# A fused attention and expert kernel: residual and router logits in one VectorE operation, GpSimd's power ahead of its scatters, first norms on ScalarE

## The chip, the cores and the metric

One core of one Trainium2 chip runs the whole program in one launch. The metric is the device time of that launch in microseconds. The engines named below are TensorE (PE in the profile, PEld for its weight loads), VectorE (DVE), ScalarE (ACT), GpSimd (POOL) and SyncE (SP), each with its own queue of instructions that it works through in order. Where one engine needs what another has made, it waits on a semaphore.

## The reference

The input x is 4 sequences of 1024 tokens of 128 numbers, float32. One layer is computed:

```
n  = layernorm(x)                       # over the 128 numbers, eps 1e-5
s  = (n Wq^T)(n Wk^T)^T / sqrt(1024)    # one head, causal
x1 = x + softmax(s) (n Wv^T) Wo^T
m  = layernorm(x1)
p  = softmax(m G^T)                     # 8 experts; the two best of each token
y  = sum over the two: p_e * (silu(m W1_e) * (m W3_e)) W2_e     # hidden width 256
out = x1 + y
```

## The kernel before

**Tiles and slots.** The 4096 tokens are 32 tiles of 128. The attention part runs in slots s = -3 to 31, one tile a slot, in two halves: tiles 0 to 15 are two sequences, 16 to 31 the other two. Within a half tile u has `blocks(u) = u % 16 // 2 + 1` blocks of 128 keys, so slots grow from 1 block to 8 and start again at 1 in slot 16. Wq and Wk are folded into one 128x128 matrix (`A_sb`) ahead of time, Wv, Wo and the router's weights into another (`M_sb`). Each engine's order is written out by hand, and the parts of one tile are spread over slots:

- PE, slot s: transpose of the normed tile s+3 (`transposes`, L536), scores of tile s+1 (L546, and the mask L547), projections of tile s+2 (`projections`, L559 and L560), transposes of the probabilities of tile s (`turn`, L569), in every fourth slot the ranks of a group of four tiles (L583 to L588), then probabilities times values of tile s-1 (`weigh`, L595). The last gives 136 columns: 128 of the attention's output and 8 that are its share of the router's logits.
- ACT, slot s: copies PSUM to SBUF: `XX` (L744, the transposed normed tile), `TL` (L749) and `xg` (L751, the logits' share of x itself, scaled by the standard deviation `sd1`), `PT` (L759), then the exponentials `Pr` of tile s+1 (L765, with a read of the row sum). PE's L559 of slot s waits for `XX` of slot s.
- DVE, slot s: for tile s-2 the reciprocal of the row sum (L879), the residual `X` (L885), the logits (L890, `gate`), mean and variance (L895, L899, `ve2` L903); for tile s+12 the first statistics (L850, L854; up to slot 19); for tile s+4 the first norm `xn` (L864); the negated maximum of the scores of tile s+1 (L874); the second norm of tile s-3 into `rows` (L911); the best experts (L917, L921); every fourth slot the routing of a group (L928 to L940) and a slot later the places of its rows (L948 to L982, ending in the semaphore `row_rdy`); in slots 22 to 26 also pieces of the list of expert tiles (L996 to L1024).
- POOL: the power -0.5 of the variances, four first ones at a time (`rstd1`, L398) and one second one a slot (`rstd2`, L402, for tile s-2), and the indirect DMAs that scatter the normed rows to the experts' stretches in DRAM (L451): 8 for each group of four tiles, queued in `waiting` when the group's places are known.

DVE's L911 in slot s needs `rstd2` of tile s-3, which POOL makes in its slot s-1. PE's `weigh` of tile u waits for the logits of tile u-1, since both use one PSUM bank.

**After slot 31** the expert part runs in 72 tiles of 128 rows: SP loads the rows, PE multiplies by W1 and W3 (L648) and W2 (L666), ACT makes silu (L781) and stages weights (L776), DVE multiplies (L1079, L1086), POOL scatters the results (L460), and at the end DVE adds them to `X` (L1197), which is written out.

## Time and profile before

| what | value |
|---|---|
| median of three runs | 292.99 us (292.64 to 295.81) |
| profiled execution | 293.88 us, its span 292.0 us |
| mean granted TensorE clock | 0.959 |
| attention part, up to the last `weigh` | from 0 to about 137 us of the span |
| expert part | from about 137 us to the end |
| PE, DVE, ACT, POOL busy over the span | 83%, 67%, 47%, 58% |
| L864 `xn`, 32 times | 10.8 us, mean 345 ns |
| L890 logits, 32 times | 7.0 us, mean 217 ns |
| L451 scatters, 64 times | 64.3 us, mean 1005 ns |
| L402 `rstd2`, 32 times | 19.1 us, mean 596 ns |

Busy shares are averages over stages that have different limits. The time of an instruction in a row is from its start to its end; on DVE and ACT the next one often starts before that end, so what an instruction costs its engine is the distance from its start to the next one's start. Idle time stands in square brackets behind a row, with what ended it.

### The profile page before, as it was taken

What the parts mean: (1) busy time and instruction counts of PE and PEld (TensorE: products, weight loads), DVE (VectorE), ACT (ScalarE), POOL (GpSimd) and SP (SyncE); (2) the same over time, 40 slices, a digit from 0 to 9 for tenths busy, and PEclk for the clock granted to TensorE, in tenths of its full rate; (3) what the DMA queues carried; (4) which work ended last, traced back from release to release, by engine and by line L of the source; (5) the groups of instructions that cost most, each with busy time, mean ns of one, the idle gap of its engine ahead of it and who ended that gap; (6) DMA issues with size and microseconds to landing.
All of it is one profiled execution on the core that took longest, in us unless ns stands there. A gap on an engine that the chain in (4) does not pass through costs nothing.

```text
span 292.0 us, 6399 instructions
## 1 busy us (share of the span) xinstructions
PE 241.4 (83%) x1769; PEld 209.5 (72%) x1770; DVE 195.0 (67%) x925; ACT 137.9 (47%) x369; POOL 169.1 (58%) x214
## 2 busy tenths in 40 slices
PE   7889999999698889798696788988979969899700
PEld 7767787788476767687595678878969858899600
DVE  4569998686788997685943289556464455597531
ACT  2256665575355555466743153455355354545100
POOL 5524388846868865627665745646556535475740
PEclk9999999999979999999988879999999999999975
DMA  7997011100101112201332224333222225751773
GB/s 215 322 339 208 3 38 46 39 28 30 38 28 38 50 46 61 72 19 39 89 82 65 67 69 112 92 94 83 74 77 82 73 56 147 228 193 37 236 243 108
DMA packets 31211, 28.96 MB, mean 99 GB/s; under 512 B 4168, under 2 KB 25680, under 8 KB 31184
## 3 DMA queue, kind: packets, MB, share of 16 engines
q1 hardware_dynamic: 25216, 18.80, 23.9%
q0 software_dynamic: 4352, 9.05, 9.0%
q10 hardware_dynamic: 1616, 0.79, 1.0%
q8 instruction: 12, 0.20, 0.3%
q14 instruction: 15, 0.12, 0.2%
HBM read 16.40 MB, written 12.22 MB: 98 GB/s over the span
## 4 chain that ended last, share of the span: by engine, by line
PE 56%; DVE 14%; issue 8%; POOL 6%; ACT 5%; another core or an unknown queue 4%; DMA 4%; SPq 1%; POOLq 0%; DVEq 0%
PE scores L648 9%; PE weighed L595 7%; PE turned L648 7%; PE weighed L666 7%; PE scores L546 7%; PE mixed L666 5%; POOL expert_rows L451 3%; PE scores L640 3%; PE turned L569 3%; PE mixed L559 3%; DVE ysb L1086 2%; PE mixed L560 2%; DMA TL<-L_attn_w_v 2%; DVE g L1079 2%
## 5 line engine op out<-in xcount | busy, mean ns | idle before, releaser
L460 POOL DMA_INDIRECT choice_rows<-ysb,ycol x72 | 71.4, 992 | 51.9 <-DVE ysb L1086 33.7
L451 POOL DMA_INDIRECT expert_rows<-rows,slots x64 | 64.3, 1005 | 30.2 <-issue 15.2
L776 ACT ACTIVATE Wt<-W 128x512 f32 x72 | 44.7, 625 | 13.8 <-issue 13.8
L648 PE MATMUL scores<-xT,Wt 128*128 128x128 f32 x288 | 41.2, 289 | 5.5 <-issue 4.7
L595 PE MATMUL weighed<-TL,PT 128*128 128x136 f32 x288 | 39.8, 283 | 3.6 <-DVE logit L890 2.4
L1071 DVE COPY xT<-scores 128x128 f32<-128x128 f32 x72 | 20.5, 285 | 32.8 <-PE scores L640 19.1
L648 PEld LDWEIGHTS scores<-xT,Wt 128*128 128x128 f32 x288 | 37.4, 203 | 6.9 <-issue 5.7
L595 PEld LDWEIGHTS weighed<-TL,PT 128*128 128x128 f32 x288 | 35.8, 191 | 4.7 <-issue 2.7
L648 PE MATMUL turned<-xT,Wt 128*128 128x128 f32 x288 | 38.5, 277 | 0.0
L546 PE MATMUL scores<-XX,TL 128*128 128x512 f32 (+3 forms) x96 | 37.6, 501 | 1.0 <-ACT TL L749 1.0
L648 PEld LDWEIGHTS turned<-xT,Wt 128*128 128x128 f32 x288 | 35.5, 194 | 0.0
L402 POOL TENSOR_TENSOR rstd<-ve,halves 128x1 f32<-128x1 f32 x32 | 19.1, 596 | 21.4 <-DVE ve L903 20.3
L666 PE MATMUL weighed<-w_sb,g 128*128 x148 | 25.0, 294 | 6.9 <-DVE ysb L1086 6.8
L781 ACT ACTIVATE sil<-turned 128x256 f32<-128x256 f32 x36 | 13.8, 383 | 35.4 <-PE turned L648 16.9
L749 ACT ACTIVATE TL<-mixed 128x264 f32<-128x264 f32 x32 | 12.5, 391 | 35.9 <-PE mixed L560 31.6
L765 ACT ACTIVATE Pr<-scores,negmax 128x128 f32<-128x128 f32 (+7 forms) x32 | 23.9, 747 | 7.1 <-DVE negmax L874 6.2
L666 PEld LDWEIGHTS weighed<-w_sb,g 128*128 128x128 f32 x148 | 20.5, 201 | 8.9 <-issue 8.7
L874 DVE TENSOR_REDUCE negmax<-scores 128x1 f32<-128x128 f32 (+7 forms) x32 | 23.5, 735 | 4.9 <-PE scores L547 3.7
L781 ACT ACTIVATE sil<-scores 128x256 f32<-128x256 f32 x36 | 13.7, 380 | 24.6 <-PE scores L648 16.9
L640 PE MATMUL scores<-identf,xt 128*128 128x128 f32 x72 | 19.9, 283 | 6.0 <-DVE xT L1071 6.0
L666 PE MATMUL mixed<-w_sb,g 128*128 x140 | 22.9, 287 | 2.4 <-DVE ysb L1086 1.9
L759 ACT ACTIVATE PT<-turned 128x512 f32<-128x512 f32 (+3 forms) x48 | 22.0, 491 | 3.1 <-PE turned L569 2.9
(145 smaller groups left out, 439.7 us busy)
## 6 DMA issues: line engine op xcount, KB each, us to landing
xt<-expert_rows SPq DMA_DIRECT2D x72, 66.0 KB
XX<-choice_rows SPq DMA_DIRECT2D x16, 256.0 KB
W<-L_ffn_w SPq DMA_DIRECT2D x2, 1024.0 KB, 9.6
choice_rows<-ysb,ycol POOLq DMA_INDIRECT x72
X<-L_attn_in_features SPq DMA_DIRECT2D x2, 512.0 KB, 8.0
expert_rows<-rows,slots POOLq DMA_INDIRECT x64
out<-X SPq DMA_DIRECT2D x4, 256.0 KB
expert_rows<-padrows SPq DMA_DIRECT2D x1, 528.0 KB
```

The source lines that it names most:

```text
L451: nc.gpsimd.indirect_dma_start(xs, bass.IndirectOffsetOnAxis(ap=slots[:, u, k:k + 1], axis=0), rows[:, u % ROWS_RING, k, :], None).then_in ...
L460: nc.gpsimd.indirect_dma_start(yb, bass.IndirectOffsetOnAxis(ap=ycol[:, q, 0:1].bitcast(u32), axis=0), ysb[:, q, :], None).then_inc(y_out[ ...
L546: mm(pS[u % 2][:, c:c + n * P], TL[:, u, 0:P], keys, start=True, stop=c + 512 < w)
L595: i = mm(pO[:, 0:VG], PT[:, u % 2, kt * P:(kt + 1) * P], TL[:, keys_of(u)[0] + PAIR * kt, P:], start=kt == 0, stop=kt == blocks(u) - 1)
L640: nc.tensor.transpose(bank[j % 2][:, 0:P], xt[:, j, 0:D], identf[:, :]).then_inc(xT_mm, 1)
L648: i = mm(bank[2 + j % RING][:, c * P:(c + 1) * P], Wt[:, j % RING, c * P:(c + 1) * P], xT[:, j % RING, :], start=True, stop=True)
L666: i = mm(product_bank(m, j)[:, 0:D], g[:, j % RING, c * P:(c + 1) * P], w2_sb[:, ds(w + c * D, D)], start=c == 0, stop=c == H // P - 1)
L759: copy(PT[:, u % 2, 4 * c * P:4 * c * P + w], pT[n % 2][:, 0:w], ACT.Copy).then_inc(pt_ev, 1)
L765: copy(Pr[:, u % 2, 0:w], pS[u % 2][:, 0:w], ACT.Exp, bias=negmax[:, u:u + 1], scale=1.0, accum_out=rowsum[:, u:u + 1]).then_inc(p_rdy, 1)
L776: copy(Wt[:, j % RING, :], W[:, ds(w * (SET // WIDE), SET)], ACT.Copy).then_inc(Wt_rdy, 1)
L781: copy(sil[:, j % RING, :], bank[2 + j % RING][:, 0:H], ACT.Silu).then_inc(sil_rdy, 1)
L874: v.tensor_reduce(negmax[:, u:u + 1], pS[u % 2][:, 0:blocks(u) * P], AX.X, ALU.max, negate=True).then_inc(max_rdy, 1)
```

## The change

Four things are done.

**1. One operation for residual and logits.** `X` gets rows of 136 columns; ACT writes `xg` into the last 8 of them, and one DVE operation adds all 136 columns. `gate` and the tile `logit` are gone. The semaphore `logit_rdy` is replaced by `x1_rdy`. Loads, stores and the last additions read the first 128 columns of each row.

**2. First norms on ScalarE.** The first four `xn` stay on DVE. The other 28 become an ACT operation, Identity with scale `rstd1` and bias `shift1` = -mean * rstd, at the end of ACT's slot (tile s+5, slots -1 to 26). DVE makes `shift1` for four tiles at once (L879 of the new file), beside `sd1`.

**3. GpSimd's power first.** `rstd_2` stands ahead of the slot's first scatter.

**4. Fewer scatters in short slots.** The second scatter of a slot (the one that waits for `pt_ev`) is made only where the slot has more than 4 blocks.

```diff
-        X = sb("X", [P, N_TILES, D])
+        X = sb("X", [P, N_TILES, VG])
...
+                if is_tile(s - X1_LAG):
+                    rstd_2(s - X1_LAG)
                 if waiting and is_tile(s):
                     pool.wait_ge(xx_ev, n_xx(s))
                     scatter(*waiting.pop(0))
-                if is_tile(s - X1_LAG):
-                    rstd_2(s - X1_LAG)
...
-                if waiting and is_tile(s):
+                if waiting and is_tile(s) and blocks(s) > 4:
                     pool.wait_ge(pt_ev, chunks(s + 1))
                     scatter(*waiting.pop(0))
...
-                wait(pe, logit_rdy, u)
+                wait(pe, x1_rdy, u)
...
-                copy(xg[:, u, :], pM[:, P + VG:P + VG + E], ACT.Copy, scale=sd1[:, u:u + 1]).then_inc(xg_rdy, 1)
+                copy(X[:, token_tile(u), D:], pM[:, P + VG:P + VG + E], ACT.Copy, scale=sd1[:, u:u + 1]).then_inc(xg_rdy, 1)
+
+            def norm1(u):
+
+                act.wait_ge(shift1_rdy, u // STAT1_GROUP + 1)
+                act.wait_ge(xx_mm, n_xx(u - 4 - XT_LEAD))
+                copy(xn[:, u % 4, :], X[:, token_tile(u), 0:D], ACT.Identity, bias=shift1[:, u:u + 1],
+                     scale=rstd1[:, u:u + 1]).then_inc(xn_rdy, 1)
...
                     exps(s + S_LEAD)
+                if s >= -1 and is_tile(s + NORM1_LEAD + 1):
+                    norm1(s + NORM1_LEAD + 1)
...
+                v.scalar_tensor_tensor(out=shift1[:, t], in0=mv1[:, t, 0], scalar=-1.0, in1=rstd1[:, t],
+                                       op0=ALU.mult, op1=ALU.mult).then_inc(shift1_rdy, 1)
...
-                v.scalar_tensor_tensor(out=X[:, token_tile(u), :], in0=pO[:, 0:D], scalar=rinv[:, u:u + 1],
+                dve.wait_ge(xg_rdy, u + 1)
+                v.scalar_tensor_tensor(out=X[:, token_tile(u), :], in0=pO[:, 0:VG], scalar=rinv[:, u:u + 1],
                                        in1=X[:, token_tile(u), :], op0=ALU.mult, op1=ALU.add).then_inc(x1_rdy, 1)
-
-            def gate(u):
-                dve.wait_ge(xg_rdy, u + 1)
-                v.scalar_tensor_tensor(out=logit[:, u, :], in0=pO[:, P:VG], scalar=rinv[:, u:u + 1],
-                                       in1=xg[:, u, :], op0=ALU.mult, op1=ALU.add).then_inc(logit_rdy, 1)
...
                     attend(u2)
-                    gate(u2)
...
-                if s >= 0 and is_tile(s + NORM1_LEAD):
-                    norm1(s + NORM1_LEAD)
-                    if (s + NORM1_LEAD) % STAT1_GROUP == 0:
-                        spread1(s + NORM1_LEAD)
+                if s == -S_LEAD:
+                    spread1(STAT1_GROUP)
+                u4 = s + NORM1_LEAD + 3
+                if u4 > STAT1_GROUP and is_tile(u4) and u4 % STAT1_GROUP == 0:
+                    spread1(u4)
```

How it moves instructions is seen in three places. The first is POOL in slots 15 and 16, before:

```order
L398 TENSOR_TENSOR rstd<-ve,halves 128x4 [waits ve1_rdy]
L451 DMA expert_rows<-rows,slots 34816x132 [waits xx_ev]
L402 TENSOR_TENSOR rstd<-ve,halves 128x1 [waits ve2_rdy]
L451 DMA expert_rows<-rows,slots 34816x132 [waits pt_ev]
L451 DMA expert_rows<-rows,slots 34816x132 [waits p_rdy]
L451 DMA expert_rows<-rows,slots 34816x132 [waits xx_ev]
L402 TENSOR_TENSOR rstd<-ve,halves 128x1 [waits ve2_rdy]
```

and in the changed kernel:

```order
L398 TENSOR_TENSOR rstd<-ve,halves 128x4 [waits ve1_rdy]
L402 TENSOR_TENSOR rstd<-ve,halves 128x1 [waits ve2_rdy]
L451 DMA expert_rows<-rows,slots 34816x132 [waits xx_ev]
L451 DMA expert_rows<-rows,slots 34816x132 [waits pt_ev]
L451 DMA expert_rows<-rows,slots 34816x132 [waits p_rdy]
L402 TENSOR_TENSOR rstd<-ve,halves 128x1 [waits ve2_rdy]
L451 DMA expert_rows<-rows,slots 34816x132 [waits xx_ev]
```

Each `rstd` of one column has moved ahead of the scatter in front of it. In slots 16 to 23 one scatter a slot is left of two; those left out run in slots 24 to 30, three a slot.

The second is ACT in slot 2 and the start of slot 3 (`XX` is the copy for which PE's L559 waits), before:

```order
L749 ACTIVATE TL<-mixed 128x264 [waits tl_mm]
L751 ACTIVATE xg<-mixed,sd1 128x8 [waits sd1_rdy]
L759 ACTIVATE PT<-turned0 128x256 [waits pt_mm]
L765 ACTIVATE Pr,rowsum<-scores1,negmax 128x256 [waits max_rdy]
L744 ACTIVATE XX<-scores1 128x128 [waits xx_mm]
```

and in the changed kernel:

```order
L749 ACTIVATE TL<-mixed 128x264 [waits tl_mm]
L751 ACTIVATE X<-mixed,sd1 128x8 [waits sd1_rdy]
L766 ACTIVATE PT<-turned0 128x256 [waits pt_mm]
L772 ACTIVATE Pr,rowsum<-scores1,negmax 128x256 [waits max_rdy]
L757 ACTIVATE xn<-X,shift1,rstd1 128x128 [waits xx_mm,shift1_rdy]
L744 ACTIVATE XX<-scores1 128x128 [waits xx_mm]
```

The new norm stands between the exponentials and the next `XX`.

The third is DVE in slot 21, before:

```order
L879 RECIPROCAL rinv<-rowsum 128x1
L885 SCALAR_TENSOR_TENSOR X<-weighed,rinv,X 128x128
L890 SCALAR_TENSOR_TENSOR logit<-weighed,rinv,xg 128x8
L895 BN_STATS bn<-X 128x6
L864 TENSOR_SCALAR xn<-X,mv,rstd 128x128
L899 BN_AGGR mv<-bn 128x2
L874 TENSOR_REDUCE negmax<-scores 128x1
```

and in the changed kernel:

```order
L889 RECIPROCAL rinv<-rowsum 128x1
L896 SCALAR_TENSOR_TENSOR X<-weighed,rinv,X 128x136
L901 BN_STATS bn<-X 128x6
L878 TENSOR_TENSOR sd<-ve,rstd 128x4
L879 SCALAR_TENSOR_TENSOR shift<-mv,rstd 128x4
L905 BN_AGGR mv<-bn 128x2
L884 TENSOR_REDUCE negmax<-scores 128x1
```

Two instructions are gone from between the residual, its statistics and their aggregate; two small ones stand there in every fourth slot. PE's order is the same in both kernels.

## Rows read from the trace of the kernel before

**Rows 1.** Windows: us, busy PE, PEld, DVE, ACT, POOL (instructions), PEclk, DMA, GB/s

```profile
44.00:59.00 15.00, 14.52 (x100) 11.35 (x98) 11.89 (x60) 7.96 (x24) 12.28 (x15) 1.00 0.13 42
88.00:104.00 16.00, 14.08 (x95) 10.70 (x93) 14.50 (x79) 8.64 (x28) 13.27 (x16) 1.00 0.14 44
```

**Rows 2.** Chain of waits, 12 to 36 us: start, us, what

```profile
22.55 0.18 ACT XX L744
...
24.93 0.18 ACT XX L744
```

**Rows 3.** Timeline, ACT: start, us, engine, line, operation, shapes

```profile
17.64 0.38 ACT L765 ACTIVATE Pr<-scores,negmax 128x128 f32<-128x128 f32 x1
17.99 0.30 ACT L744 ACTIVATE XX<-scores 128x128 f32<-128x128 f32 x1
```

**Rows 4.** Timeline, ACT's XX and PE's L559 in slots 5 and 7

```profile
27.29 0.29 ACT L744 ACTIVATE XX<-scores 128x128 f32<-128x128 f32 x1
27.64 0.49 PE L559 MATMUL mixed<-XX,A_sb 128*128 128x128 f32 x2
...
32.91 0.28 ACT L744 ACTIVATE XX<-scores 128x128 f32<-128x128 f32 x1
33.79 0.30 PEld L559 LDWEIGHTS mixed<-XX,A_sb 128*128 128x128 f32 x2
```

**Rows 5.** Chain of waits, 66 to 78 us

```profile
74.43 0.96 POOL expert_rows L451
...
75.69 0.96 POOL expert_rows L451
...
76.68 0.58 POOL rstd L402
...
77.28 0.41 DVE rows L911
```

**Rows 6.** Timeline, DVE in slots 20 to 22 and 28

```profile
85.18 0.22 DVE L890 SCALAR_TENSOR_TENSOR logit<-weighed,rinv,xg 128x8 f32<-128x8 f32 x1
85.31 0.28 DVE L895 BATCH_NORM_STATS2 bn<-X 128x6 f32<-128x128 f32 x1
85.51 0.33 DVE L864 TENSOR_SCALAR xn<-X,mv,rstd 128x128 f32<-128x128 f32 x1
85.76 0.16 DVE L870 TENSOR_TENSOR sd<-ve,rstd 128x4 f32<-128x4 f32 x1
...
87.25 0.47 DVE L911 TENSOR_SCALAR rows<-X,mv,rstd 128x256 f32<-128x256 f32 x1 [0.74 <-POOL rstd L402]
...
90.32 0.48 DVE L911 TENSOR_SCALAR rows<-X,mv,rstd 128x256 f32<-128x256 f32 x1 [0.50 <-POOL rstd L402]
...
92.74 0.28 DVE L895 BATCH_NORM_STATS2 bn<-X 128x6 f32<-128x128 f32 x1
...
93.18 0.17 DVE L899 BATCH_NORM_AGGREGATE mv<-bn 128x2 f32<-128x6 f32 x1
...
118.31 0.35 DVE L885 SCALAR_TENSOR_TENSOR X<-weighed,rinv,X 128x128 f32<-128x128 f32 x1 [2.96 <-remote]
...
118.71 0.28 DVE L895 BATCH_NORM_STATS2 bn<-X 128x6 f32<-128x128 f32 x1
119.02 0.18 DVE L899 BATCH_NORM_AGGREGATE mv<-bn 128x2 f32<-128x6 f32 x1
```

**Rows 7.** Timeline, PE in slots 11 and 31, where DVE keeps it

```profile
47.48 0.30 PE L536 MATMUL mixed<-identf,xn 128*128 128x128 f32 x1 [0.41 <-issue]
...
132.11 2.09 PE L595 MATMUL weighed<-TL,PT 128*128 128x136 f32 x16 [0.36 <-DVE logit L890]
```

**Rows 8.** Timeline, POOL's power in slots 24, 25 and 32

```profile
102.04 0.57 POOL L402 TENSOR_TENSOR rstd<-ve,halves 128x1 f32<-128x1 f32 x1
...
106.39 0.61 POOL L402 TENSOR_TENSOR rstd<-ve,halves 128x1 f32<-128x1 f32 x1
...
135.76 0.58 POOL L402 TENSOR_TENSOR rstd<-ve,halves 128x1 f32<-128x1 f32 x1
```

More of the change, by code:

```diff
@@ L124, in build @@
         gsum, gmean = sb("gsum", [E, 1]), sb("gmean", [E, 1])
-        sd1, xg, logit = sb("sd1", [P, N_TILES]), sb("xg", [P, N_TILES, E]), sb("logit", [P, N_TILES, E])
+        sd1, shift1 = sb("sd1", [P, N_TILES]), sb("shift1", [P, N_TILES])
         identf, identb = sb("identf", [P, P]), sb("identb", [P, P], bf16)
@@ L198, in build @@
         xg_rdy = sem("xg_rdy")
-        sd1_rdy, logit_rdy, dtop_rdy = sem("sd1_rdy"), sem("logit_rdy"), sem("dtop_rdy")
+        sd1_rdy, shift1_rdy, dtop_rdy = sem("sd1_rdy"), sem("shift1_rdy"), sem("dtop_rdy")
         woT_lo_rdy, woT_hi_rdy = sem("woT_lo_rdy"), sem("woT_hi_rdy")
@@ L290, in _ @@
             xv = x.rearrange("b (i p) d -> p b i d", p=P)
-            Xv = X[:, :, :].rearrange("p (b i) d -> p b i d", b=B)
+            Xv = X[:, :, 0:D].rearrange("p (b i) d -> p b i d", b=B)
             sp.dma_start(wo_sb, w_o).then_inc(wo_in, 16)
@@ L357, in write @@
                 for n, z in pieces(c):
-                    sp.dma_start(ov[:, n:n + z, :], X[:, n:n + z, :]).then_inc(out_done, 16)
+                    sp.dma_start(ov[:, n:n + z, :], X[:, n:n + z, 0:D]).then_inc(out_done, 16)
             def after_load(t):
@@ L662, in down @@
                     if t == 0:
-                        pe.wait_ge(logit_rdy, N_TILES)
+                        pe.wait_ge(x1_rdy, N_TILES)
                 for c in range(H // P):
@@ L841, in _ @@
                 for n, z in pieces(c):
-                    act.dma_start(ov[:, n:n + z, :], X[:, n:n + z, :]).then_inc(out_done, 16)
+                    act.dma_start(ov[:, n:n + z, :], X[:, n:n + z, 0:D]).then_inc(out_done, 16)
         @block.vector
@@ L849, in stats1 @@
             def stats1(u):
-                v.bn_stats(bn1[:, u, :], X[:, token_tile(u), :]).then_inc(bn1_rdy, 1)
+                v.bn_stats(bn1[:, u, :], X[:, token_tile(u), 0:D]).then_inc(bn1_rdy, 1)
             def aggregate1(u):
@@ L862, in norm1 @@
                 dve.wait_ge(rstd1_rdy, u // STAT1_GROUP + 1)
-                wait(dve, xx_mm, n_xx(u - 4 - XT_LEAD) if u >= 4 else 0)
-                v.tensor_scalar(xn[:, u % 4, :], X[:, token_tile(u), :], mv1[:, u, 0:1], rstd1[:, u:u + 1],
+                v.tensor_scalar(xn[:, u % 4, :], X[:, token_tile(u), 0:D], mv1[:, u, 0:1], rstd1[:, u:u + 1],
                                 ALU.subtract, ALU.mult).then_inc(xn_rdy, 1)
@@ L884, in attend @@
                 dve.wait_ge(pv_mm, u + 1)
[L885 removed]
+                dve.wait_ge(xg_rdy, u + 1)
+                v.scalar_tensor_tensor(out=X[:, token_tile(u), :], in0=pO[:, 0:VG], scalar=rinv[:, u:u + 1],
                                        in1=X[:, token_tile(u), :], op0=ALU.mult, op1=ALU.add).then_inc(x1_rdy, 1)
[L888 to L891 removed]
             def stats2(u):
                 dve.wait_ge(x1_rdy, u + 1)
[L895 removed]
+                v.bn_stats(bn2[:, u, :], X[:, token_tile(u), 0:D]).then_inc(bn2_rdy, 1)
             def aggregate2(u):
@@ L911, in norm2 @@
                 v.tensor_scalar(rows[:, u % ROWS_RING, :, 0:D],
-                                X[:, token_tile(u):token_tile(u) + 1, :].to_broadcast([P, K, D]),
+                                X[:, token_tile(u):token_tile(u) + 1, 0:D].to_broadcast([P, K, D]),
                                 mv2[:, u, 0:1], rstd2[:, u:u + 1], ALU.subtract, ALU.mult).then_inc(x2_rdy, 1)
             def top_values(u):
-                dve.wait_ge(logit_rdy, u + 1)
-                v.max(top[:, u, :], logit[:, u, :]).then_inc(top_rdy, 1)
+                dve.wait_ge(x1_rdy, u + 1)
+                v.max(top[:, u, :], X[:, token_tile(u), D:]).then_inc(top_rdy, 1)
             def top_experts(u):
                 dve.wait_ge(top_rdy, u + 1)
-                v.max_index(topi[:, u, :], top[:, u, :], logit[:, u, :]).then_inc(topi_rdy, 1)
+                v.max_index(topi[:, u, :], top[:, u, :], X[:, token_tile(u), D:]).then_inc(topi_rdy, 1)
             def route(gr):
@@ L1184, in _ @@
                     list_full(part)
-            pairs = X[:, :, :].rearrange("p (n t) d -> p n (t d)", t=2)
+            pairs = X[:, :, 0:D].rearrange("p (n t) d -> p n t d", t=2)
             def add_choice(c, k):
                 a, apart = CHUNKS[c]
-                Xc = pairs[:, a // 2:a // 2 + apart // 2 + 1:apart // 2, :]
+                Xc = pairs[:, a // 2:a // 2 + apart // 2 + 1:apart // 2, :, :]
                 if k == 0:
@@ L1196, in add_choice @@
                     dve.wait_ge(sum0, c + 1)
-                v.tensor_tensor(Xc, Xc, yf[:, c % ZF, k, :, :].rearrange("p (n t) d -> p n (t d)", t=2),
+                v.tensor_tensor(Xc, Xc, yf[:, c % ZF, k, :, :].rearrange("p (n t) d -> p n t d", t=2),
                                 ALU.add).then_inc([sum0, sum1][k], 1)
```

1 line of the change is left out of this document (removed).

## The prediction, made before the changed kernel ran

> **What bounds the kernel now.** I read the chain of waits first, since busy shares mislead here: VectorE is busy 14.50 of 16 us in one stretch and 11.89 of 15 in another, while TensorE is at 14 or more in both [rows 1]. The chain changes its owner four times before the expert part. From 12 to 25 us (slots -1 to 4) it runs in a loop between ScalarE and TensorE: `XX`, TensorE's L559 and L560, `TL`, `xg`, `PT`, `Pr`, the next `XX`, 2.38 us a turn at slot 4 [rows 2]; VectorE is not on it. From there to 63.5 us every piece is TensorE's: VectorE's idle time in slots 12 to 15 costs nothing. Then ScalarE's last exponentials of the half release VectorE's row places, these release GpSimd's scatters, and from 67 to 77.3 us the chain is GpSimd's: scatter behind scatter, the power, and VectorE's L911 that waits for it [rows 5]. From 77 to 104 us it is VectorE's, with two waits for GpSimd's power inside it, 0.74 and 0.50 us [rows 6]. From 104 us it is TensorE's again. So the reader should ask of each edit in which of these stages it sits.
>
> **The change part by part.** The sum is made on the profiled execution (293.88 us, span 292.0); it lies 0.89 us above the median of 292.99, and I put the same difference on both.
>
> *The norm on ScalarE, first half: a loss.* It stands between `Pr` and `XX`, so in slots where `XX` is on the chain it adds its whole price. No row has a ScalarE operation with scale and bias from memory and no accumulator. The nearest below is `XX` itself, 0.18 us of the chain [rows 2]; the nearest above is a 128-column `Pr`, from whose start to the next start, with the read of its accumulator, 0.35 us pass [rows 3]. It lacks that read but has one more operand, so I take 0.30, nearer to `Pr`. The `XX` of slots 0 to 4 pay it in full: 5 x 0.30 = 1.50. In slot 5 `XX` ends at 27.58 and TensorE is free at 27.64 [rows 4], which leaves 0.24; slot 6 is alike, 0.22. In slot 7 `XX` ends at 33.19 and L559 starts at 33.79 [rows 4]: 0.6 us of cover, and from there the norm is hidden. Loss 1.96 us. Of this 0.41 comes back in slot 11, where TensorE waits for VectorE's row places [rows 7]: VectorE will be early there and TensorE late. Together +1.55 us.
>
> By the Trainium skill (ScalarE: Activation LUTs, "What ACT_TABLE_LOAD costs") such an ACTIVATE takes 186 ns, 93 ns for each pointer operand and 0.833 ns an element, and overlaps its neighbour by 93 ns: an estimate of 0.37 us. By it this part would be about 0.5 us dearer and the total 291.4 us.
>
> *Power first, fewer scatters: a gain.* Scatters follow each other every 1.26 us [rows 5]. On the chain from 67.7 us to the power that L911 waits for at 77.28, exactly one scatter fewer stands ahead of the power of slot 16; the five of slots 14 and 15 stay. That is -1.27, and +0.30 because the norm of ScalarE's slot 14 delays the exponentials of the group that release those scatters: -0.97 us. Behind it, slots 16 to 23 now hold one scatter each, GpSimd needs about 2.1 us a slot and VectorE more than that, so the waits of 0.74 and 0.50 us [rows 6] go: -1.24 us.
>
> *VectorE's two operations: a gain, but a smaller one than their times.* The logits cost their queue 0.13 us (85.18 to 85.31) and the norm 0.25 us (85.51 to 85.76) [rows 6], not the 0.22 and 0.33 that the rows show. And both cover waits: statistics wait for the end of the residual, 0.35 us, and start 0.40 after its start even behind the logits; their aggregate comes 0.44 us after them with the norm between and 0.31 us without it (slot 28, which has none) [rows 6]. So a slot gives 0.02 + 0.13 = 0.15 us, not 0.38. It counts in slots 18 to 26, where VectorE leads: 9 x 0.15 = 1.35 us. In slots 2 to 17 it gives nothing: the chain is elsewhere. `shift1` falls into the same gap ahead of the aggregate; the 8 extra columns are some 0.01 us. At slot 31 `weigh` waits for the logits [rows 7]; now it waits for the residual itself, 0.13 us less.
>
> The Trainium skill (VectorE: DVE Perf Modes, "The DRAIN you can't avoid") says that the next operation does not start until the pipe is empty. By that each slot would give the full 0.22 + 0.33 us, and the sum would be 287.3. The rows above, with starts 0.13 us apart behind an operation of 0.22, speak against it.
>
> *Costed at nothing:* the norm on ScalarE in slots 7 to 13 (covered by TensorE's scores) and in 18 to 26 (there ScalarE waits for VectorE's maximum; in slots 19 to 21 its own loop of 2.4 to 2.6 us would grow to 2.7 to 2.9 while VectorE needs 2.2 to 3.3, so the cover is thin); the wider rows of `X` in loads, stores and last additions (same pieces of 512 bytes, same number of elements); the expert part, whose instructions are the same.
>
> *Sum:* +1.55 - 0.97 - 1.24 - 1.35 - 0.13 = -2.1 us: 291.7 for an execution like the profiled one, **290.9 us** for the median. With the norm at 0.18 it is 289.9, at 0.35 it is 291.2; if TensorE takes the lead two slots earlier than I think, 0.3 more. Own range 289.6 to 291.9.
>
> **Rivals.**
>
> *VectorE gives the full distances* (the waits behind the residual shrink as well): 9 x 0.38 instead of 9 x 0.15, 288.8 us. For it: VectorE is almost without gaps there. Against: slot 28 shows the gap [rows 6]. Chance 0.12.
>
> *The stall goes.* At 118.31 VectorE, and TensorE and ScalarE with it, came out of a standstill of 2.96 us [rows 6], while SyncE issued the loads of the first expert rows. These now start about two slots later, since the fifth group's last scatter moves from slot 25 to 27. If the stall came from that meeting, up to 2.9 us of it may go: with half of it, 289.4; with all, 288.0. It may as well only move. Chance 0.10.
>
> *GpSimd's backlog.* The scatters left out come back: slots 24 to 30 hold three each. Such a slot takes GpSimd 4.35 us (102.04 to 106.39), eight of them 34.8 us, and the same stretch took 33.7 (102.04 to 135.76) [rows 8]. So GpSimd falls behind by 1.1 us and some 0.5 more for the slots that shorten, against a cover of nearly a slot. With scatters of 1.4 us (several rows of 1.16 to 1.5 exist) 22 of them add 2.9 us, which is more than the cover leaves, and VectorE's L911 waits again: about +1.5, 292.4 us. Chance 0.13.
>
> *Slower: ScalarE's loop is the bound of all short slots.* If the norm costs 0.48 us (its whole duration, nothing overlapped), the first half loses 7 x 0.48 - 0.2 - 0.4 = 2.8, GpSimd's stretch gives 0.8, and in slots 19 to 23 a turn of 2.9 to 3.5 us is as long as VectorE's slot was with its waits, which leaves 0.5 of the gains there. Total +1.5: 294.5 us. It decides from about 0.45 us a norm. Chance 0.12.
>
> The rest, 0.05, is for what I do not see. My forecast has 0.48.
>
> **Numbers.** The likeliest is 290.9. The range runs from the stall's half and VectorE's full price to the slower rival: 288.4 to 294.4. A change of 1% is 2.9 us and about what a measurement of this kernel tells from none: below 290.06 lies 0.14 of the forecast, 0.11 of the first rival, 0.08 of the second: 0.33. Above 295.9 lies the far end of the slower rival, of the backlog and of the rest: 0.08. Between them 0.59.
>
> **What would show it.** The norm: the chain's turn from `XX` to `XX` at slot 4 grows from 2.38 to about 2.68 us, and the chain still runs through ScalarE there; slot 11 shows no wait of L536. GpSimd: L911 of slot 17 starts about 10 us after ScalarE's last `Pr` of 1024 columns ends, a microsecond sooner than now, and L911 waits for the power nowhere in slots 18 to 31. VectorE: statistics 0.38 us behind the residual, aggregate 0.31 behind them. I would be wrong if `XX` in slots 0 to 4 is not the piece that releases TensorE, if L911 waits for `rstd` in slots 26 to 31, or if L559 in slots 19 to 22 sits behind `XX` while VectorE idles.

## The result: 0.7% slower, on that chip

Against the kernel before, run beside it on the same chip, the changed kernel takes 298.26 us to 295.33 (medians of 20 runs each): a ratio of 1.0072, 95% interval 1.0037 to 1.0107, some 2.1 us slower. The ratio leaves out runs of the slower state and is not the quotient of the two medians; the profiled execution of the changed kernel (298.32 us, span 296.5) is such a slow run and that of the kernel before is not, so a difference between these two traces counts only where the later traces of the changed kernel have it too. Put on the 292.99 us that the forecast started from, the ratio gives 295.1 us: neither the sign (-2.1 us was forecast) nor the range (-4.6 to +1.4 us) held it. It lies in the band within 1% of before, which the prediction gave 0.59.

| us | before | after |
|---|---|---|
| VectorE busy | 195.0 | 190.6 |
| ScalarE busy | 137.9 | 147.6 |
| residual of slot 2 to that of slot 9 | 20.33 | 21.83 |
| 9 to 11 | 8.48 | 10.48 |
| 11 to 17 | 25.59 | 25.51 |
| 17 to 22 | 18.40 | 14.73 |
| 22 to 26 | 15.76 | 16.26 |
| 26 to 30 | 18.19 | 20.11 |
| 30 to 33 | 13.97 | 13.30 |
| from there to the end | 151.8 | 153.2 |

The stretches are differences between the starts of VectorE's residual operation on `X` (L885 before, L896 after; each slot has one). A slot's number is that of its last residual: "slot 11" below is the stretch from the residual of slot 10 to that of slot 11. Ahead of slot 2 lie another 1.59 us, of which 0.84 are already there at TensorE's first L559 (13.71 us against 12.87). I put them to no edit: in three traces of the kernel before, the residual of slot 2 starts at 19.5, 20.1 and 20.5 us.

Two more traces of the changed kernel (a0 and a1, in the table of stretches below) repeat the differences of 2 to 9, of 17 to 22 and of slot 23. Those of 9 to 11 and of 26 to 30 are in a0 too, and hardly or not in a1.

The chain of waits of the changed kernel, 22 to 30 us (start, us, what), answers to [rows 2]:

```profile
22.26 0.18 ACT XX L744
...
24.54 0.38 ACT xn L757
24.91 0.18 ACT XX L744
25.09 0.04 issue
25.13 0.49 PE mixed L559 x2
...
27.29 0.38 ACT xn L757
27.67 0.18 ACT XX L744
```

The turn at slot 4 is 2.76 us, the norm 0.38 of it. The timeline answers to [rows 4]; L559 now waits where it had been covered:

```profile
30.76 0.49 PE L559 MATMUL mixed<-XX,A_sb 128*128 128x128 f32 x2 [0.31 <-ACT XX L744]
```

In the second run of short slots the chain (84 to 100 us) has left VectorE for the same loop:

```profile
87.81 0.19 ACT Pr L772
88.01 0.38 ACT xn L757
88.39 0.18 ACT XX L744
88.61 0.49 PE mixed L559 x2
...
96.92 0.38 ACT xn L757
97.30 0.13 ACT elog L793
97.45 0.19 DVE esum L976
```

Its last three rows are a second price: `elog` stands behind the norm, VectorE's row places wait for it, and slot 23 takes 5.09 us instead of 4.20. The windows answer to [rows 1] (us, then busy PE, PEld, DVE, ACT, POOL, PEclk, DMA, GB/s): ScalarE has 10.92 of 16 us, GpSimd 9.06 instead of 13.27, and in the first window TensorE, the bound there, works 13.57 us instead of 14.52.

```profile
44.00:59.00 15.00, 13.57 (x95) 10.79 (x93) 11.28 (x52) 8.75 (x26) 11.79 (x14) 1.00 0.12 41
88.00:104.00 16.00, 14.28 (x98) 11.16 (x99) 14.14 (x73) 10.92 (x37) 9.06 (x12) 1.00 0.07 23
```

TensorE's timeline shows what it does with that time. It had done `turned` (0.82 us from 48.37), and the ranks came 1.12 us after it had no work left that the profile knows:

```profile
48.37 0.82 PE L569 MATMUL turned<-identf,Pr 128*128 128x128 f32 x6
50.30 0.18 PE L584 MATMUL mixed<-seen,onesb 128*128 128x32 bf16 x1 [1.12 <-issue]
```

VectorE got these ranks at 51.86, after 1.15 us of waiting. I call this a stop: TensorE's rows stand still, or its releases come one to three microseconds late (up to five in other places), with no work of the kernel ahead of them. The trace of before has one in slot 28 [rows 6] and none here.

### The profile page after: what moved, and what is told of

Same layout as the page of the kernel before. It is cut to its first block, busy times and chain, and to the rows that moved or that the text cites. A ratio compares the mean times of both kernels' runs of the same rounds, so it can differ in the third digit from the quotient of the medians.

```text
span 296.5 us, 6375 instructions
## 1 busy us (share of the span) xinstructions
PE 244.0 (82%) x1769; PEld 212.6 (72%) x1770; DVE 190.6 (64%) x873; ACT 147.6 (50%) x397; POOL 168.8 (57%) x214
## 4 chain that ended last, share of the span: by engine, by line
PE 51%; DVE 15%; ACT 11%; issue 11%; another core or an unknown queue 6%; DMA 3%; ACTq 1%; POOL 1%; POOLq 0%; SPq 0%; DVEq 0%
PE scores L648 8%; PE weighed L595 7%; PE turned L648 6%; PE scores L546 5%; PE weighed L666 5%; PE mixed L666 5%; PE mixed L559 4%; PE turned L569 3%; ACT Pr L772 3%; PE scores L640 3%; DVE ysb L1092 3%; PE mixed L560 2%; DVE g L1085 2%; ACT PT L766 2%
## 5 line engine op out<-in xcount | busy, mean ns | idle before, releaser
L460 POOL DMA_INDIRECT choice_rows<-ysb,ycol x72 | 71.5, 993 | 53.8 <-DVE ysb L1092 37.7
L648 PE MATMUL scores<-xT,Wt 128*128 128x128 f32 x288 | 42.1, 294 | 3.9 <-issue 2.2
L1077 DVE COPY xT<-scores 128x128 f32<-128x128 f32 x72 | 20.5, 285 | 35.7 <-PE scores L640 15.9
L648 PEld LDWEIGHTS scores<-xT,Wt 128*128 128x128 f32 x288 | 38.4, 207 | 5.1 <-issue 2.8
L648 PE MATMUL turned<-xT,Wt 128*128 128x128 f32 x288 | 39.2, 280 | 0.0
L546 PE MATMUL scores<-XX,TL 128*128 128x512 f32 (+3 forms) x96 | 36.9, 493 | 1.4 <-ACT TL L749 1.0
L648 PEld LDWEIGHTS turned<-xT,Wt 128*128 128x128 f32 x288 | 36.1, 197 | 0.0
L666 PE MATMUL weighed<-w_sb,g 128*128 x148 | 26.1, 303 | 6.7 <-DVE ysb L1092 6.7
L788 ACT ACTIVATE sil<-turned 128x256 f32<-128x256 f32 x36 | 13.8, 383 | 32.4 <-PE scores L648 10.3
L666 PEld LDWEIGHTS weighed<-w_sb,g 128*128 128x128 f32 x148 | 21.7, 211 | 9.5 <-issue 9.4
L666 PEld LDWEIGHTS mixed<-w_sb,g 128*128 128x128 f32 x140 | 19.7, 203 | 7.0 <-issue 6.9
```

The source lines that it names most:

```text
L460: nc.gpsimd.indirect_dma_start(yb, bass.IndirectOffsetOnAxis(ap=ycol[:, q, 0:1].bitcast(u32), axis=0), ysb[:, q, :], None).then_inc(y_out[ ...
L546: mm(pS[u % 2][:, c:c + n * P], TL[:, u, 0:P], keys, start=True, stop=c + 512 < w)
L648: i = mm(bank[2 + j % RING][:, c * P:(c + 1) * P], Wt[:, j % RING, c * P:(c + 1) * P], xT[:, j % RING, :], start=True, stop=True)
L666: i = mm(product_bank(m, j)[:, 0:D], g[:, j % RING, c * P:(c + 1) * P], w2_sb[:, ds(w + c * D, D)], start=c == 0, stop=c == H // P - 1)
L788: copy(sil[:, j % RING, :], bank[2 + j % RING][:, 0:H], ACT.Silu).then_inc(sil_rdy, 1)
L1077: v.tensor_copy(xT[:, j % RING, :], bank[j % 2][:, 0:P]).then_inc(xT_rdy, 1)
```

## The experiments

Each time is compared with the kernel before on the same chip. The chips turned out to be of two kinds, told apart by the median time of the unchanged kernel before: 267.5 and 267.9 us on two chips ("quick"), 294.9 to 299.7 us on three others and 295.3 us in the first comparison ("slow"). The table holds all timed runs, as the ratio to before and its 95% interval. One of the eleven runs of the changed kernel with norms on VectorE on a slow chip took 473.37 us; it is unexplained and not in its ratio. No run profiled the kernel before on a quick chip, so a part's stretches there can be set only against those of other parts.

| kernel | quick chips | slow chips |
|---|---|---|
| changed | 0.9961 (0.9928, 0.9993) | 1.0072 (1.0037, 1.0107); 1.0110 (1.0081, 1.0140) |
| GpSimd's part alone | 0.9886 (0.9844, 0.9928) | 1.0085 (1.0049, 1.0121) |
| ScalarE's norm alone | 1.0094 (1.0059, 1.0128) | 1.0090 (1.0052, 1.0129) |
| merged operation alone | 0.9961 (0.9932, 0.9991) | 0.9932 (0.9897, 0.9967) |
| changed, norms on VectorE | 0.9834 (0.9794, 0.9875); 0.9809 (0.9775, 0.9843) | 1.0033 (0.9998, 1.0068) |
| changed, norm between XX and TL | 0.9816 (0.9776, 0.9855) | 0.9980 (0.9951, 1.0008) |
| the same from tile 18 on | 0.9820 (0.9787, 0.9852) | 0.9984 (0.9946, 1.0023) |
| norms on VectorE, spare norms on ScalarE | not run | 1.0274 (1.0230, 1.0318) |

The stretches between residuals, in us, of one profiled execution each:

| kernel | 2-9 | 9-11 | 11-17 | 17-22 | 22-26 | 26-30 | 30-33 | rest |
|---|---|---|---|---|---|---|---|---|
| slow: before (b1) | 20.33 | 8.47 | 25.58 | 18.34 | 16.06 | 18.16 | 14.62 | 152.8 |
| norm alone (e2b) | 22.31 | 8.83 | 25.60 | 17.95 | 15.56 | 18.26 | 13.95 | 151.7 |
| merged alone (e3b) | 20.21 | 8.48 | 25.59 | 18.05 | 15.84 | 17.89 | 13.94 | 150.7 |
| GpSimd alone (e1b) | 19.91 | 10.46 | 25.11 | 15.48 | 15.87 | 21.37 | 13.46 | 153.9 |
| norms on VectorE (e4c) | 19.79 | 10.43 | 25.06 | 15.24 | 15.86 | 20.75 | 12.68 | 151.9 |
| changed (a0) | 21.81 | 11.66 | 25.40 | 15.59 | 16.27 | 20.86 | 14.09 | 154.5 |
| quick: norm alone (e2) | 22.34 | 8.67 | 25.76 | 17.96 | 15.59 | 16.34 | 13.95 | 126.0 |
| merged alone (e3) | 20.19 | 8.46 | 25.57 | 18.02 | 15.86 | 16.50 | 13.67 | 125.2 |
| GpSimd alone (e1) | 19.92 | 8.55 | 24.83 | 16.04 | 15.86 | 16.49 | 13.95 | 127.4 |
| norms on VectorE (e4b) | 19.79 | 8.66 | 24.83 | 15.74 | 15.87 | 16.48 | 13.70 | 125.7 |
| changed (a1) | 21.82 | 9.13 | 24.62 | 15.39 | 16.27 | 16.41 | 13.67 | 125.6 |
| norm between XX and TL (e5b) | 19.71 | 8.76 | 24.82 | 15.16 | 15.27 | 16.34 | 13.73 | 125.1 |

### One part at a time (a quick chip)

GpSimd's part alone:

```diff
+                if is_tile(s - X1_LAG):
+                    rstd_2(s - X1_LAG)
                 if waiting and is_tile(s):
                     pool.wait_ge(xx_ev, n_xx(s))
                     scatter(*waiting.pop(0))
-                if is_tile(s - X1_LAG):
-                    rstd_2(s - X1_LAG)
...
-                if waiting and is_tile(s):
+                if waiting and is_tile(s) and blocks(s) > 4:
```

> The kernel before with GpSimd's part of the change alone: the power ahead of the first scatter, and no scatter behind the PT evictions of slots with four blocks or fewer. Theory N (the loss is ScalarE's norm: its loop carries 0.38 us more a turn in the short slots, and GpSimd's part is a gain): 1.0 to 2.2 us faster than before, the span from the X of slot 16 to that of slot 18 about 1.2 us shorter (8.55 us in the trace of before), and VectorE's rows of slots 18 to 22 wait for the power nowhere. Rival G (the backlog of scatters that is put off to slots 24 to 30 costs more than is gained): 1 us or more slower than before, lost behind slot 23.

Measured: 264.88 us to 267.46, 1.1% faster. Rival G fell, and theory N has the sign and the places, though the gain by the ratio, 3.0 us, is more than its 2.2. Slots 17 and 18 take 7.64 us (8.54 in the first trace of before, 8.87 in the merged operation's trace on the same chip), and VectorE waits for the power nowhere in slots 18 to 22. The backlog costs nothing here: the stretch 26 to 30, where the backlog sits, is 16.49 us, with no more of it than in the kernels without the backlog (16.34 and 16.50).

The norm alone:

```diff
+            def norm1(u):
+                act.wait_ge(shift1_rdy, u // STAT1_GROUP + 1)
+                act.wait_ge(xx_mm, n_xx(u - 4 - XT_LEAD))
+                copy(xn[:, u % 4, :], X[:, token_tile(u), :], ACT.Identity, bias=shift1[:, u:u + 1],
+                     scale=rstd1[:, u:u + 1]).then_inc(xn_rdy, 1)
...
                     exps(s + S_LEAD)
+                if s >= -1 and is_tile(s + NORM1_LEAD + 1):
+                    norm1(s + NORM1_LEAD + 1)
```

> The kernel before with the norms of tiles 7 and up on ScalarE alone, and shift1 for them. Theory N: 2 to 4 us slower than before: the turn from XX to XX at slot 4 is 2.76 us (2.38 before), as in the changed kernel, and the X of slot 16 comes 3 to 4 us later. Rival G or rival M (the merged operation or the wide rows of X cost the time): within 1 us of before.

Measured: 270.49 us, 0.9% or 2.5 us slower, at the low end; the later run on a slow chip gave the same 0.9%. Counted from slot 2, the residual of slot 16 comes 1.8 us later than in the first trace of before (52.9 us behind it, 51.1 there), not 3 to 4.

The merged operation alone (`X` with 136 columns a tile, `gate` gone, all readers cut to `0:D`):

```diff
-                v.scalar_tensor_tensor(out=X[:, token_tile(u), :], in0=pO[:, 0:D], scalar=rinv[:, u:u + 1],
+                dve.wait_ge(xg_rdy, u + 1)
+                v.scalar_tensor_tensor(out=X[:, token_tile(u), :], in0=pO[:, 0:VG], scalar=rinv[:, u:u + 1],
```

> The kernel before with residual and logits in one operation alone (X with 136 columns a tile, the final sums over rows with a gap). Theory N: between 1.5 us faster and no difference, its gain in slots 18 to 26 at 0.15 us a slot, little before slot 16. Rival M (the residual now waits for xg too, and every operation on X reads rows that are 544 bytes apart; the final additions have one more dimension): 1 to 3 us slower than before, in the slots or in the last additions.

Measured: 266.20 us, 0.4% faster. Rival M fell. The gain is not where theory N put it: 17 to 26 takes 33.9 us on both kinds of chip, 34.2 to 34.4 in the three traces of before, 0.3 to 0.5 us where 1.35 was expected. The 0.15 us a slot was the price of both operations; the logits' own share in the prediction is 0.02.

Both gains together, that is the changed kernel with its norms on VectorE (`norm1` of ScalarE and `shift1` out, `norm1` of slot s back in VectorE's slot s):

> The changed kernel with the norms back on VectorE (so GpSimd's part and the merged operation together). Theory N: 1.5 to 3.5 us faster than the kernel before and 3.5 to 5.5 us faster than the changed one. Rival G or M: no faster than before. Rival S (the times move with where the stalls of the instruction supply fall, not with the parts): no order among the four that the parts explain, and differences of the trace that sit in idle times of 1 to 4 us outside the slots that an edit touches.

Measured: 263.51 us, 1.7% or 4.4 us faster, more than the 1.5 to 3.5 expected. Rival S fell here: all four stand in theory N's order, and the differences sit in the slots that each edit touches.

### The place of the norm (a slow chip)

> The kernel before, unedited, for its trace beside the others of this call. Every theory: within 0.5% of the kernel before. The four X times that matter (slots 2, 10, 18, 33) as in its first trace, counted from slot 2 (24.3, 59.6 and 120.7 us behind it), but for idle times that no edit touches, such as the 2.96 us ahead of the X of slot 28.

> The changed kernel, unedited, beside the kernel before and in one call with its variants. The parts alone gave -2.6, +3.0 and -1.3 us against before. If they add up (theory N as far as it goes): 0.5 to 1.5 us faster than before, and the +2.1 us of the first comparison were partly the chip's. If they work on each other (theory I: with ScalarE's longer loop as the bound of the short slots, what VectorE and GpSimd give is no longer on the path): 1 to 3 us slower, with the turns of slots 2 to 5 at 2.65 to 2.87 us, slot 7 at 4.53 and slot 23 near 5.1 (4.22 with the norm moved alone).

The kernel before took 299.72 us here (ratio 0.9994, interval 0.995 to 1.0037), the changed one 302.37, 1.1% slower: the first result again, and on its face theory I. The turns are as expected (2.65 to 2.87, slot 7 at 4.52, slot 23 at 5.09), but they are the same on a quick chip. What a quick chip does not have is slot 11 with 7.02 us (4.62 before) and slot 27 with 6.72 (4.42).

```diff
                 if has_xx(s):
                     out_xx(s)
...
+                if s >= 0 and is_tile(s + NORM1_LEAD):
+                    norm1(s + NORM1_LEAD)
                 if has_tl(s):
                     out_tl(s)
...
-                if s >= -1 and is_tile(s + NORM1_LEAD + 1):
-                    norm1(s + NORM1_LEAD + 1)
```

> The changed kernel with ScalarE's norm moved from the end of its slot to between XX and TL, where ScalarE waits 0.82 us for TensorE in each short slot (for tile s + 4 in slot s). Theory N (the cost is the place of the norm in ScalarE's loop, not its length): the 0.51 us norm starts some 0.2 us behind XX and lies in that wait, the turn at slot 4 is back at 2.5 us or less from X to X (2.88 in the changed kernel), and the time is 4.5 to 7 us under the changed kernel's, 0 to 1.5 us under that of the version with its norms on VectorE (1.66% under before). Rival L (it is ScalarE's load, 10 us more of it, wherever it stands): no more than 1 us faster than the changed kernel.

Measured: 299.10 us, 3.3 us under the changed kernel and not the 4.5 to 7 expected. The mechanism is as theory N has it. ScalarE's timeline in slot 4 (of the later run on a quick chip; start, us, then in brackets the idle time before and its releaser):

```profile
24.69 0.30 ACT L744 ACTIVATE XX<-scores 128x128 f32<-128x128 f32 x1
24.85 0.52 ACT L757 ACTIVATE xn<-X,shift,rstd 128x128 f32<-128x128 f32 x1
25.81 0.39 ACT L749 ACTIVATE TL<-mixed 128x264 f32<-128x264 f32 x1 [0.45 <-PE mixed L560]
```

and of the version with its norms on VectorE:

```profile
24.38 0.30 ACT L744 ACTIVATE XX<-scores 128x128 f32<-128x128 f32 x1
25.50 0.39 ACT L749 ACTIVATE TL<-mixed 128x264 f32<-128x264 f32 x1 [0.83 <-PE mixed L560]
```

From `XX` to `TL` 1.12 us pass with the norm as without it; it has taken 0.38 us of a wait of 0.83. The stretch 2 to 9 is back at 19.72 us (21.81 in the changed kernel), and rival L, at most 1 us, falls. In the traces the slots up to 33 give 4.4 us against the changed kernel, and 0.9 us of it is gone again behind them. That the version is no faster than before lies elsewhere: slots 10 and 11 take 11.77 us, as in the changed kernel (11.66), against 8.55 before.

The spare norms (same shape, same place at the end of the slot, into a tile that nobody reads; VectorE keeps its own):

```diff
+            def spare_norm(u):
+                act.wait_ge(rstd1_rdy, u // STAT1_GROUP + 1)
+                copy(spare[:, u % 4, :], X[:, token_tile(u), 0:D], ACT.Identity, bias=mv1[:, u, 0:1],
+                     scale=rstd1[:, u:u + 1])
```

> The changed kernel with the norms back on VectorE, and beside them a norm of the same shape on ScalarE at the end of each slot, into tiles that nobody reads: nothing is taken from VectorE, only the operation added to ScalarE's slot. Theory N: all of the loss is that place in ScalarE's loop, so this is as slow as the changed kernel or up to 1.5 us slower (VectorE's relief is missing), 4 to 6 us slower than the version without the spare norms. Rival D (the loss is that tile u's norm now comes late for TensorE's transpose, a hand-over between engines and not the occupation): the spare norms cost under 1.5 us.

Measured: 308.47 us, 6.1 us over the changed kernel and 8.8 over before, more than theory N said. Its stretch 2 to 9 is 21.96 us, the changed kernel's 21.81: there the whole loss is the occupation of ScalarE at that place, and rival D falls. The rest of the excess lies behind slot 26, mostly in two stretches where this execution has stops (22.08 us in 26 to 30, 17.54 in 30 to 33). All six runs (304.9 to 309.3 us) lie above the changed kernel's slowest (303.8), so the excess is real; where it lies I know from one execution, and I do not explain it.

### Again on a quick chip, with a split

> The changed kernel once more, unedited, beside three of its variants in one call. On the chips of its first runs it took 0.7% and 1.1% more than before, and TensorE stood still for about 2.4 us in slots 10 and 11 (5.95 and 7.01 us for slot 11, 4.54 and 4.61 before). If that stop belongs to the kernel's order wherever it runs, it is here too; if it belongs to the chips on which the kernel before takes 293 to 300 us, it is here only if the kernel before takes that long.

> The changed kernel with its norms back on VectorE, a second time, now beside the changed kernel. Theory N: 3.5 to 6.5 us faster than the changed kernel, 1 to 2% faster than before, the turns of slots 3 to 5 at 2.26, 2.50 and 2.50 us. On the stop in slots 10 and 11: absent if the norms among ScalarE's instructions bring it (theory F), present where the changed kernel has it if GpSimd's order or the merged operation does.

> The changed kernel with ScalarE's norm between XX and TL, a second time, beside the changed kernel and the version with its norms on VectorE. Theory N: slots 18 to 22 about 1.1 us shorter than with the norms on VectorE (14.65 against 15.74 us in the traces so far), slots 3 to 9 within 0.4 us of it; where no stop of TensorE tells them apart, 0.5 to 1.5 us faster. With the stop of slots 10 and 11 it comes out 1 to 2 us slower than that version.

> The same as the last, but the norms of tiles 7 to 17 on VectorE and only those from tile 18 on by ScalarE between XX and TL: ScalarE takes them only where VectorE is the bound (slots 18 to 22). Theory N: the X of slots 2 to 17 as with all norms on VectorE, slots 18 to 22 as with all on ScalarE (14.65 us): the fastest of the four, 0.7 to 1.5 us under the version with its norms on VectorE. Theory F (each norm on ScalarE brings the stop of slots 10 and 11 with it): no stop there, wherever the changed kernel has one. Rival: the time of the second half does not follow the first (the loop over the experts starts at a time of its own): all four differ there by less than their X of slot 33 does.

The kernel before took 267.91 us, the changed one 266.64: 0.4% **faster**. The sum of its parts there is -1.1 + 0.9 - 0.4 = -0.6%. With the norms on VectorE 262.41 us (4.2 under the changed kernel), with the norm between `XX` and `TL` 263.38, with the split 262.93. The stretches with the norm between `XX` and `TL` are shorter than with the norms on VectorE (17 to 22: 15.16 against 15.74 us, 22 to 26: 15.27 against 15.87, together 1.2 us). The 1.1 us that theory N wanted in 17 to 22 alone had set a slow chip's 14.65 against a quick chip's 15.74; like against like it is 0.6 on both kinds. Its times did not come: both versions were to be 0.5 to 1.5 us faster than the norms on VectorE, and their medians are 1.0 and 0.5 us slower, with intervals that overlap. No stop is in slots 10 and 11 in any of them, so these belong to the slow chips, and theory F was not tested.

### Which part brings the stop (slow chips)

> The kernel before, unedited, for its trace. Where it takes about 267 us, no wait of ScalarE or VectorE for a late release of TensorE over 1 us (the 2.6 to 3.1 us of slot 28 in its first two traces are missing), and from the X of slot 2 to that of slot 33 about 118 us. Where it takes 293 to 300 us, those of slot 28 again, and 120.7 to 122.2 us.

> The changed kernel with its norms back on VectorE, a third time. On a chip where before takes 293 to 300 us: theory F (the stop of slots 10 and 11 comes with the norms among ScalarE's instructions) has no such stop and 1.5 to 2% under before; theory G2 (it comes with GpSimd's order or the merged operation) has 2 to 3 us in slots 10 and 11 and at best 1% under before. On a chip where before takes about 267 us: 1.7 to 1.9% under it again, as on the two before, and nothing is told of the stop.

> The norm on ScalarE alone, a second time. It was 0.94% slower than before where before took 267 us, with 4.74 us for slot 11. Theory F: where before takes 293 to 300 us it has the stop of slots 10 and 11 (6 to 7 us for slot 11) and is 1.5 to 2.5% slower; theory G2: no stop there, 1% slower.

> Norms from tile 18 on by ScalarE between XX and TL, those ahead on VectorE, with GpSimd's part and the merged operation, a second time. Theory F: no stop in slots 10 and 11 on any chip, 1.5 to 2.2% under before; theory G2: the stop where before takes 293 to 300 us, and at best 1% under before.

> GpSimd's part alone, a second time. On a chip where before takes 293 to 300 us: theory P (the power ahead of the scatter, which moves the scatters of slots 9 and 10 later, brings TensorE's stop) has 2 to 3 us more in slots 10 and 11 together (8.47 us before) and is at best 0.5% under before; theory M2 (the merged operation brings it) has none there and is 1% under before, as where before takes 267 us. On a chip of the quick kind: 1.1% under before again.

> The merged operation alone, a second time. On a chip where before takes 293 to 300 us: theory M2 has TensorE's stop in slots 10 and 11 (2 to 3 us) and is 0.5 to 1% slower than before; theory P has none there and is 0.4% under before. On a chip of the quick kind: 0.4% under before again.

The kernel before took 294.88 us beside the first four and 295.34 beside the last two; unedited again (b1) it took 296.52 (1.0028, interval 0.998 to 1.0075) and has its stop in slots 28 and 29. Theory F fell: the norm alone has 8.83 us in slots 10 and 11, while the norms on VectorE leave 10.43. Theory P held, M2 fell: the merged operation alone has 8.48 us there and stays faster (0.7%), GpSimd's part alone has 10.46 and is 0.85% **slower**, where on a quick chip it was 1.1% faster. The merged operation ran beside it on the same chip, so the chip alone does not make the difference. TensorE in slots 10 and 11 of GpSimd's part alone:

```profile
46.47 0.82 PE L569 MATMUL turned<-identf,Pr 128*128 128x128 f32 x6
48.50 0.18 PE L584 MATMUL mixed<-seen,onesb 128*128 128x32 bf16 x1 [1.22 <-issue]
```

and of the same kernel on a quick chip, where the ranks follow at once:

```profile
45.65 0.82 PE L569 MATMUL turned<-identf,Pr 128*128 128x128 f32 x6
46.54 0.18 PE L584 MATMUL mixed<-seen,onesb 128*128 128x32 bf16 x1
```

The longest stop of this trace's attention part is in slot 30 (8.13 us; 4.58 in b1). The engines that wait for TensorE come out of it within 1.5 us of each other:

```profile
129.46 0.35 DVE L885 SCALAR_TENSOR_TENSOR X<-weighed,rinv,X 128x128 f32<-128x128 f32 x1 [3.53 <-remote]
...
130.09 1.63 PE L595 MATMUL weighed<-TL,PT 128*128 128x136 f32 x12 [1.44 <-issue]
...
130.89 1.09 ACT L759 ACTIVATE PT<-turned 128x512 f32<-128x512 f32 x2 [4.87 <-remote]
```

From its stretches against b1 (one execution each, of two slow chips): it wins 0.42 us to slot 9, 0.47 in 11 to 17, 2.86 in 17 to 22, 0.19 in 22 to 26 and 1.16 behind slot 30, together 5.1; it loses 1.99 in slots 10 and 11 and 3.21 in 27 to 30, together 5.2. So the slots come out even where 2.2 us of gain were forecast. Another 1.1 us are lost in the expert part and 0.75 ahead of slot 2; whether these belong to the part, one pair of executions can't tell. The two losing stretches do belong to it: in the seven slow-chip traces with GpSimd's part 9 to 11 takes 10.4 to 11.8 us and 26 to 30 takes 20.1 to 22.1, in the five without it 8.5 to 8.8 and 17.9 to 18.7. On quick chips both ways give 8.5 to 9.1 and 16.3 to 16.5.

What the stop is stays open. In each slow-chip trace with GpSimd's part slot 9 takes 2.7 to 3.0 us; in those without the part it takes 3.3, 0.39 us of it a wait of VectorE for GpSimd's power, and there is no stop. So it could hang on what TensorE has had to do just before, or on where the scatters now fall; nothing I ran changes one without the other. Nor are the two edits of this part told apart, the order of the power and the fewer scatters: both were always made together, and both work already in slots 7 to 10 (slot 7 has four blocks, so its second scatter goes too: the first scatter starts at 35.56 us in b1 and at 39.36 in GpSimd's part alone). One candidate, a late supply of instructions, has this trace against it: the queues that the profile calls `instruction` have no packet between 46 and 49 us or between 125 and 135 us of GpSimd's part alone, where both stops lie. What moves there are scatters of rows and, in the second window, loads of the first expert rows.

## Why the prediction was wrong, step by step

*The norm's place and price: the right mechanism, mis-sized.* "I take 0.30, nearer to `Pr`": the start of `XX` comes 0.38 us after the start of the norm. By the Trainium skill (ScalarE: Activation LUTs, "What ACT_TABLE_LOAD costs") I had an estimate of 0.37; its figures for 128 columns and two pointer operands in fact add up to an estimate of 0.39 (186 + 2 x 93 + 107 - 93 ns), and the trace's 0.38 agrees with it. My row without a second memory operand was the wrong neighbour. The larger miss was "from there the norm is hidden": in slot 7, and again in slot 23, `exp_logits` stands behind the norm and VectorE's row places behind that. In the changed kernel's trace on a quick chip:

```profile
35.75 0.49 ACT L757 ACTIVATE xn<-X,shift,rstd 128x128 f32<-128x128 f32 x1
36.13 0.22 ACT L793 ACTIVATE elog<-dlog 128x32 f32<-128x32 f32 x1
...
36.39 0.19 DVE L976 TENSOR_REDUCE esum<-elog 128x4 f32<-128x32 f32 x1 [0.78 <-ACT elog L793]
```

Slot 7 takes 4.54 us there and 3.49 with the norms on VectorE; slot 23 takes 5.09 and 4.26. I had followed `XX` past the norm and not the other operation behind it. Nor did the 0.41 us of slot 11 come back: with the norm moved alone, 9 to 11 takes 8.67 us against 8.48 before. From slot 2 to 17 the norm costs 2.4 us in the traces (56.8 against 54.4), where my terms for slots 3 to 11 come to 0.65. The kernel with the norm moved alone also has VectorE's relief in it, so by my own terms it was to be 1.55 - 9 x 0.13 = +0.4 us; it measured +2.5 (1.6 to 3.4) on a quick chip and +2.7 on a slow one. That is the second miss.

*The thin cover in slots 19 to 21:* costed at nothing, and the chain runs there. On a quick chip 17 to 26 takes 31.61 us with the norms on VectorE, 30.44 with the norm between `XX` and `TL`, and 31.66 in the changed kernel. So VectorE's relief is real, 1.17 us, just the 9 x 0.13 of the forecast, but the place behind `Pr` takes all of it back: 0.2 us in 17 to 22, through ScalarE's loop, and 1.0 in slot 23, through `elog`.

*Power first, fewer scatters: the step that failed.* The mechanism is right: with this part VectorE waits for the power nowhere in slots 18 to 31, its L917 of slot 17 (L911 before) starts 10.3 us behind the end of ScalarE's last `Pr` of the half instead of 11.2, as forecast, and no wait of L917 shows the backlog. Forecast -0.97 - 1.24 = -2.2 us; on a quick chip the part gives -3.0 (-4.2 to -1.9). But I put it down as a gain wherever it runs, and on a slow chip it is +2.5 us (0.85% of 295.34). Stops of TensorE that the trace of before does not have, or has shorter, at those places cost 5.2 us there and eat up what the part wins in the slots; where the rest of the 2.5 us lies stays open. I saw one such stop, 2.96 us [rows 6], and priced only that it might go. That it could come, or come back elsewhere, I gave half a sentence ("It may as well only move") and no price, though nothing in the trace tied it to its place. This term turned the sign: on slow chips the three parts alone give +2.5 + 2.7 - 2.0 = +3.2 us, and the changed kernel +2.1 and +3.3; with this term at its forecast the sum would be -1.5. On a quick chip the changed kernel is 0.4% faster where 0.7% was forecast, and that closeness is luck: by my terms the three parts were to give -2.2, +0.4 and -0.3 us, and they gave -3.0, +2.5 and -1.0.

*VectorE's two operations:* forecast -1.35 - 0.13 us. The norm's share, 9 x 0.13, is the 1.17 us above; the logits' share, 9 x 0.02 + 0.13 = 0.3, was too small: the merged operation alone gives -1.0 (-1.8 to -0.2) on a quick chip and -2.0 (-3.0 to -1.0) on a slow one. The slots show 0.3 to 0.5 of it in 17 to 26 and, on the quick chip, 0.14 each in slots 32 and 33; the rest I have not placed. The full distances of the first rival would have given 9 x 0.38 = 3.4 us in 18 to 26. The Trainium skill (VectorE: DVE Perf Modes, "The DRAIN you can't avoid") says that the next operation does not start until the pipe is empty, and also that one that is not held starts earlier. The rows agree with the second. In slot 21 of the changed kernel on a quick chip:

```profile
88.45 0.36 DVE L896 SCALAR_TENSOR_TENSOR X<-weighed,rinv,X 128x136 f32<-128x136 f32 x1
88.85 0.29 DVE L901 BATCH_NORM_STATS2 bn<-X 128x6 f32<-128x128 f32 x1
89.06 0.14 DVE L878 TENSOR_TENSOR sd<-ve,rstd 128x4 f32<-128x4 f32 x1
89.12 0.15 DVE L879 SCALAR_TENSOR_TENSOR shift<-mv,rstd 128x4 f32<-128x4 f32 x1
89.19 0.18 DVE L905 BATCH_NORM_AGGREGATE mv<-bn 128x2 f32<-128x6 f32 x1
```

Statistics start 0.40 us behind the residual (0.38 forecast) and the aggregate 0.34 behind them (0.31 forecast); `shift` and `sd` lie in that gap, 0.06 and 0.07 us each.

*The slower rival* had the right place, ScalarE's loop in all short slots, with too high a price (0.48 us); at 0.38 it alone does not make the whole change slower, as the quick chip shows. *The backlog* showed no wait of VectorE, but its slots, 24 to 30, are where the second group of stops sits; that it brings them is not shown. (The scatters of 1.4 to 1.5 us that its price rests on are those of the expert part, L460; of the 64 meant here none takes over 1.30 us in the trace of before.)

**The best version.** With the norm between `XX` and `TL`, with the split or with the norms on VectorE, the kernel is 1.7 to 1.9% under before on quick chips and cannot be told from it on slow chips. The merged operation alone is the only one found faster on both (0.4 and 0.7%).

## What to carry to other kernels

An operation that moves to another engine costs what stands behind it there, all of it: look for the longest wait of that engine in the loop and put it there; here 0.38 us a turn went to nothing by moving it to where that engine waits 0.83 us. Follow every operation behind the new one, not only the one on the chain. And a trace with unexplained standstills is a trace of one chip: give each saving ahead of them a chance to be taken back there, and try a change of one per cent on more than one chip.
